# Reordering the pieces of pipelined local-attention layers, scores of one head unit beside values of another

## The reference

```python
def attn_layer(x, Wqkv, qs, ksc, Wo):
    q, k, v = jnp.split(x @ Wqkv, 3, -1)          # 16 heads of 64
    q = l2norm(q) * qs;  k = l2norm(k) * ksc
    q, k = rotary(q), rotary(k)
    sim = jnp.einsum('bhwie,bhwje->bhwij', q_windows, k_windows) * 8.0
    attn = jax.nn.softmax(where(mask, -max, sim), -1)      # 64 queries see 128 keys
    return merge_heads(attn @ v) @ Wo
def ffn_layer(x, g, bln, W1, b1, W2, b2):
    xn = layernorm(x) * g + bln
    a, gate = jnp.split(xn @ W1 + b1, 2, -1)      # 682 wide each
    return a * gelu(gate) @ W2 + b2
for i in range(6):
    x = attn_layer(shift_tokens(x), ...) + x
    x = ffn_layer(shift_tokens(x), ...) + x
```

## Time and profile before

| | |
|---|---|
| median of 3 runs | 3866.04 us (3858.51 to 3867.04) |
| profiled execution, span | 3864.4 us |
| PE, PEld busy in the span | 3676.7 us, 2617.3 us |
| DVE, ACT, POOL busy | 2739.6, 2354.5, 2226.1 us |
| local layers | from about 916 us to the end |

### The profile page before, as it was taken

The page is one execution under the profiler, slowest core; times in us unless marked ns, Lnnn a source line. Parts: engine busy times, 40 slices in busy tenths (PEclk is TensorE's granted clock), DMA queues, the critical chain, the costliest instruction groups (busy, mean ns, idle before and its releaser), DMA issues.

```text
span 3864.4 us, 79529 instructions
## 1 busy us (share of the span) xinstructions
PE 3676.7 (95%) x27354; PEld 2617.3 (68%) x27354; DVE 2739.6 (71%) x9052; ACT 2354.5 (61%) x6994; POOL 2226.1 (58%) x2087
## 2 busy tenths in 40 slices
PE   8899998867899999999999999999999999999998
PEld 6566666634567776777777777777777777777776
DVE  4688878744777777777777777777777777777763
ACT  3455555533566666666676666666666667666663
POOL 1677777763665655655556556565565555655640
PEclk9899999979999999999999999999999999999999
DMA  3777787780000001001000010000100001000000
GB/s 125 181 186 185 186 184 186 185 216 28 4 4 7 30 14 33 12 7 41 6 30 14 5 41 15 23 14 4 41 15 30 7 4 41 16 29 7 4 7 28
DMA packets 111071, 211.79 MB, mean 55 GB/s; under 512 B 22321, under 2 KB 72017, under 8 KB 109137
## 3 DMA queue, kind: packets, MB, share of 16 engines
q0 software_dynamic: 40960, 134.25, 14.7%
q1 hardware_dynamic: 69568, 72.33, 5.9%
q10 hardware_dynamic: 144, 0.13, 0.0%
HBM read 192.00 MB, written 2.10 MB: 50 GB/s over the span
## 4 chain that ended last, share of the span: by engine, by line
PE 70%; issue 2%; DVE 2%; POOL 1%; ACT 1%; DMA 0%; SPq 0%; DVEq 0%; POOLq 0%; ACTq 0%
PE pj L1818 24%; PE pj L1898 12%; PE y_ps L1881 8%; PE y_ps L1907 6%; PE sc L1846 5%; PE o_ps L1872 5%; PE tp L1857 5%; PE tp L1826 4%; PE tp L1796 1%; POOL l_qk_rot L1759 0%; DVE l_probs L2131 0%; DVE l_qk_cos L2092 0%; POOL l_r_q L1764 0%; DMA l_xf<-l_stream 0%; ACT l_probs L1977 0%
## 5 line engine op out<-in xcount | busy, mean ns | idle before, releaser
L1818 PE MATMUL pj<-w_qkv,l_xT 128*128 128x512 f32 x2304 | 1063.4, 598 | 7.3 <-ACT l_qk_sq L1964 5.8
L1759 POOL TENSOR_TENSOR l_qk_rot<-l_qk_cos,l_qk_sin 128x512 f32<-128x512 f32 x376 | 555.3, 1477 | 839.2 <-DVE l_qk_sin L2095 555.8
L1818 PEld LDWEIGHTS pj<-w_qkv,l_xT 128*128 128x128 f32 x2304 | 413.5, 191 | 387.1 <-issue 372.3
L511 POOL DMA_INDIRECT f_rows<-in_emb,f_expert x512 | 506.6, 989 | 224.9 <-issue 144.0
L1977 ACT ACTIVATE l_probs<-l_probs,l_low 128x128 f32<-128x128 f32 x1536 | 594.1, 391 | 2.2 <-DVE l_low L2131 0.4
L1898 PE MATMUL pj<-l_xnT,l_w 128*128 128x256 f32 x2112 | 511.4, 387 | 2.5 <-DVE l_hT L2162 1.2
L1942 ACT ACTIVATE l_qk_raw<-pj 128x512 f32<-128x512 f32 x384 | 227.1, 591 | 431.0 <-PE pj L1818 417.6
L2085 DVE TENSOR_REDUCE l_ss<-l_qk_sq 128x8 f32<-128x512 f32 x384 | 261.3, 680 | 312.7 <-ACT l_qk_sq L1964 167.9
L2131 DVE CUSTOM_DVE_ANT_0 l_probs<-sc,l_shut,l_r_q 128x128 f32<-128x128 f32 x1536 | 440.1, 343 | 52.7 <-PE tp L1857 45.8
L1898 PEld LDWEIGHTS pj<-l_xnT,l_w 128*128 128x128 f32 x2112 | 384.2, 191 | 65.5 <-issue 17.4
L1881 PE MATMUL y_ps<-w_o,l_oT 128*128 128x256 f32 x1536 | 339.6, 379 | 3.5 <-ACT l_oT L1942 3.5
...
## 6 DMA issues: line engine op xcount, KB each, us to landing
w_qkv<-in_L_ffn_Wqkv SPq DMA_DIRECT2D x12, 1024.0 KB, 7.1
...
f_rows<-in_emb,f_expert POOLq DMA_INDIRECT x512
w_o<-in_L_ffn_Wo SPq DMA_DIRECT2D x6, 1024.0 KB, 5.5
...
l_xf<-l_stream SPq DMA_DIRECT2D x48, 128.0 KB
...
```

The costliest lines, as they stand in the source:

```text
L511: pool.indirect_dma_start(rows[:, j % RH, k, :], None, dram["emb"], bass.IndirectOffsetOnAxis(ap=expert[:, n % 2, at:at + 1], axis=0)).the ...
L1759: pool.tensor_tensor(qk_rot[:, i % ROTS, :], qk_cos[:, b, :], qk_sin[:, b, :], ALU.add).then_inc(rotated if s == 0 else pool_front, 1)
L1818: last = pe.matmul(pj[b][:, :], xT[:, k, t * P:(t + 1) * P], w_qkv[:, k, s * INNER + c * 512:s * INNER + (c + 1) * 512], start=(k == 0), s ...
```

## The change

The four tables of the local layers are replaced by others. Nothing is computed otherwise, no instruction is added or removed, and no buffer or semaphore changes; `START` is empty in the changed kernel, so that step 0 uses the vector table too. The diff, cut to one line or two of each table (all line numbers behind the tables move up by 8):

```diff
     ORDER["tensor"] = [
-        ("project", 10, 0), ... ("scores", 0, 0), ("w1", 3, -3), ("w1", 4, -3), ("turn", (2, 1), -1), ("w1", 5, -3), ("turn", (2, 0), -1), ("values", 1, -1),
+        ("w1", 3, -3), ("w1", 4, -3), ("xs", 0, 1), ("w1", 5, -3), ("turn", (2, 1), -1), ("values", 1, -1), ("scores", 0, 0), ("turn", (2, 0), -1),
...
     ORDER["vector"] = [
-        ("rotate", 6, 0), ("rotate", 7, 0), ("turn", (1, 0), -1), ("top", (3, 0), -1), ("w1", 1, -3), ("res_a", 0, -2), ("qk_turn", 2, 0),
+        ("res_a", 0, -2), ("turn", (1, 0), -1), ("rotate", 6, 0), ("qk_turn", 2, 0), ("top", (3, 0), -1), ("w1", 1, -3), ("ln_stats", 0, -2),
...
-    START["vector"] = [
-        ("rotate", 3, 0), ("qk_turn", 0, 0), ("top", (2, 1), -1), ("rotate", 4, 0), ("turn", (0, 0), -1), ("rotate", 5, 0), ("norm", 1, -1),
```

More of the change, by code:

```diff
@@ L1411, in local_layers @@
     ORDER["tensor"] = [
[L1412 to L1415, removed]
@@ L1416, in local_layers @@
-        ("project", 0, 1), ("project", 1, 1), ("turn", (3, 1), -1), ("scores", 1, 0), ("turn", (3, 0), -1), ("project", 2, 1), ("values", 2, -1),
-        ("w2", 0, -3), ("qk_turn", 7, 0), ("w2", 1, -3), ("project", 3, 1), ("qk_turn", 6, 0), ("xn", 0, -2), ("values", 3, -1), ("turn", (0, 1), 0),
-        ("w1", 0, -2), ("scores", 2, 0), ("turn", (0, 0), 0), ("qk_turn", 0, 1),
+        ("turn", (0, 0), -1), ("project", 4, 0), ("qk_turn", 1, 0), ("project", 5, 0), ("project", 6, 0), ("wo", 0, -2), ("project", 8, 0),
@@ new lines, in local_layers @@
+        ("turn", (1, 0), -1), ("turn", (1, 1), -1), ("project", 7, 0), ("project", 9, 0), ("w1", 1, -3), ("qk_turn", 3, 0), ("qk_turn", 2, 0),
+        ("scores", 3, -1), ("values", 0, -1), ("w1", 2, -3), ("project", 10, 0), ("qk_turn", 4, 0), ("project", 11, 0), ("qk_turn", 5, 0),
+        ("w1", 3, -3), ("w1", 4, -3), ("xs", 0, 1), ("w1", 5, -3), ("turn", (2, 1), -1), ("values", 1, -1), ("scores", 0, 0), ("turn", (2, 0), -1),
+        ("project", 0, 1), ("turn", (3, 0), -1), ("turn", (3, 1), -1), ("project", 1, 1), ("values", 2, -1), ("scores", 1, 0), ("project", 2, 1),
@@ L1419, in local_layers @@
+        ("qk_turn", 6, 0), ("w2", 0, -3), ("qk_turn", 7, 0), ("project", 3, 1), ("xn", 0, -2), ("w2", 1, -3), ("turn", (0, 1), 0), ("qk_turn", 0, 1),
+        ("w1", 0, -2), ("values", 3, -1), ("scores", 2, 0),
     ]
     ORDER["scalar"] = [
-        ("o_copy", 3, -2), ("project", 4, 0), ("project", 5, 0), ("project", 6, 0), ("project", 8, 0), ("qk_turn", 1, 0), ("turn", (1, 1), -1),
-        ("project", 7, 0), ("project", 9, 0), ("exp", (2, 0), -1), ("w1", 1, -3), ("exp", (2, 1), -1), ("exp", (3, 0), -1), ("qk_turn", 3, 0),
@@ L1423, in local_layers @@
[L1423 to L1426, removed]
+        ("o_copy", 3, -2), ("qk_turn", 1, 0), ("exp", (1, 1), -1), ("project", 5, 0), ("project", 6, 0), ("project", 8, 0), ("exp", (2, 0), -1),
@@ new lines, in local_layers @@
+        ("project", 7, 0), ("turn", (1, 1), -1), ("project", 9, 0), ("w1", 1, -3), ("exp", (2, 1), -1), ("w1", 2, -3), ("qk_turn", 3, 0),
+        ("exp", (3, 0), -1), ("o_copy", 0, -1), ("project", 10, 0), ("project", 11, 0), ("w1", 3, -3), ("qk_turn", 5, 0), ("exp", (3, 1), -1),
+        ("w1", 4, -3), ("xs", 0, 1), ("w1", 5, -3), ("turn", (2, 1), -1), ("gelu", 0, -3), ("project", 0, 1), ("o_copy", 1, -1), ("project", 1, 1),
+        ("exp", (0, 0), 0), ("o_copy", 2, -1), ("turn", (3, 1), -1), ("exp", (0, 1), 0), ("project", 2, 1), ("qk_turn", 7, 0), ("xn", 0, -2),
@@ L1427, in local_layers @@
+        ("project", 3, 1), ("turn", (0, 1), 0), ("exp", (1, 0), 0), ("w1", 0, -2), ("project", 4, 1),
     ]
     ORDER["vector"] = [
-        ("rotate", 3, 0), ("qk_turn", 0, 0), ("top", (2, 1), -1), ("rotate", 4, 0), ("turn", (0, 0), -1), ("rotate", 5, 0), ("norm", 1, -1),
-        ("rotate", 6, 0), ("rotate", 7, 0), ("turn", (1, 0), -1), ("top", (3, 0), -1), ("w1", 1, -3), ("res_a", 0, -2), ("qk_turn", 2, 0),
-        ("top", (3, 1), -1), ("qk_turn", 4, 0), ("w1", 2, -3), ("norm", 2, -1), ("norm", 3, -1), ("w1", 3, -3), ("w1", 4, -3), ("ln_stats", 0, -2),
@@ L1432, in local_layers @@
-        ("w1", 5, -3), ("turn", (2, 0), -1), ("top", (0, 0), 0), ("ln_apply", 0, -2), ("top", (0, 1), 0), ("gates", 0, -3), ("rotate", 0, 1),
-        ("rotate", 1, 1), ("turn", (3, 0), -1), ("rotate", 2, 1), ("res_f", 0, -3), ("norm", 0, 0), ("qk_turn", 6, 0), ("top", (1, 0), 0),
-        ("top", (1, 1), 0), ("w1", 0, -2), ("top", (2, 0), 0), ("entry", 0, 2),
+        ("rotate", 3, 0), ("top", (2, 0), -1), ("turn", (0, 0), -1), ("rotate", 4, 0), ("norm", 1, -1), ("rotate", 5, 0), ("top", (2, 1), -1),
@@ new lines, in local_layers @@
+        ("res_a", 0, -2), ("turn", (1, 0), -1), ("rotate", 6, 0), ("qk_turn", 2, 0), ("top", (3, 0), -1), ("w1", 1, -3), ("ln_stats", 0, -2),
+        ("top", (3, 1), -1), ("w1", 2, -3), ("qk_turn", 4, 0), ("norm", 2, -1), ("rotate", 7, 0), ("w1", 3, -3), ("w1", 4, -3), ("entry", 0, 2),
+        ("w1", 5, -3), ("norm", 3, -1), ("top", (0, 0), 0), ("turn", (2, 0), -1), ("ln_apply", 0, -2), ("top", (0, 1), 0), ("rotate", 0, 1),
+        ("turn", (3, 0), -1), ("gates", 0, -3), ("rotate", 1, 1), ("top", (1, 0), 0), ("qk_turn", 6, 0), ("norm", 0, 0), ("top", (1, 1), 0),
@@ L1435, in local_layers @@
+        ("rotate", 2, 1), ("res_f", 0, -3), ("w1", 0, -2), ("qk_turn", 0, 1),
     ]
     ORDER["gpsimd"] = [
-        ("rotate", 3, 0), ("rotate", 4, 0), ("rotate", 5, 0), ("rotate", 6, 0), ("rotate", 7, 0), ("rope", 0, 1), ("ln_rstd", 0, -2),
-        ("rotate", 0, 1), ("rotate", 1, 1), ("rotate", 2, 1),
+        ("rotate", 6, 0), ("rotate", 7, 0), ("ln_rstd", 0, -2), ("rope", 0, 1), ("rotate", 0, 1), ("rotate", 1, 1), ("rotate", 2, 1),
+        ("rotate", 3, 1), ("rotate", 4, 1), ("rotate", 5, 1),
```

## The result

| | before | after |
|---|---|---|
| median of 4 runs each | 3862.93 us (3858.51 to 3867.04) | 3884.87 us (3881.26 to 3890.66) |
| ratio, 95% interval | | 1.0063 [1.0048, 1.0077] |
| span of the profiled execution | 3864.4 us | 3882.2 us |

The account below looks back on a forecast made before the run. TensorE, busy throughout the steady layers, was taken to bound the kernel. Span 3864.4 - 33 - 22 + 42 + 9 + 14 = 3874.4 us; with the median 1.6 above, 3876, stated as 3875, range 3836 to 3892.

Parts of the forecast that it names:

- Pairs: TensorE, steady steps: merging scores with values saves switches and restarts, 0.75 us a step, 33 us over 44 steps.
- Beginning and end: Fill, drain and last layer: TensorE waits less, as for scores behind top (1,1); 22 us off, bounds 0 and 35.
- Steady hand-offs: Ordinary steps: new order causes no waits between engines; 0 taken, bounds 0 and 0.4 us a step (0 to 18).
- hand-offs fail in each step: Rival, ordinary steps: hand-offs lose 0.2 to 0.4 us each step on top of the forecast; 3884 to 3893, chance 0.14.
- Late copy in a layer's last step: Five steps: staged copy queues behind next layer's loads, so project 11 is 8.5 us late, 42 us in all.
- lower bound: Layer's last step, if the copy overtakes the loads: project 11 late by only 4.0 us, 20 in all.
- Second step: Layer's second step, five times: copy stands behind Wo's 1 MB, late by 1.9 us, 9 us in all (bound 0).
- Clock: TensorE after the 8.5 us wait: lower granted clock costs 2.8 us, five times, 14 us (bounds 0 and 18).
- rival that nothing is late: Staged copy causes no lateness at all, so only the gains remain: 3866 - 55 = 3811 us; chance 0.07.

Follow-up runs that it names:

- e10: Kernel before with one pair merged: scores 1 moved behind turn (3,0) and project 2, to values 2; 3868.14 us (one run) against 3878.67, step 59.70 us.
- e4: e2 with two of the four merged pairs on TensorE pulled apart; 3951.35 us, 0.9958 of the kernel before.
- e7: e1 with both VectorE moves, those of e5 and e6; 3920.06 us, 0.9858 of the kernel before.
- e2: Changed kernel with the staged copy issued first in SP's step, ahead of both loads; 3932.68 us, 0.9910 of the kernel before.
- e1: Changed kernel with ln_stats back behind w1 4 on VectorE; 3928.14 us, 0.9887 of the kernel before.
- e5: e1 with VectorE's copy of turn (2,0) ahead of top (0,0); 3938.04 us (one run) against 3980.12 for the kernel before, step 59.47 us.
- e6: e1 with turn (3,0) and gates ahead of two rotate on VectorE; 3932.20 us (one run) against 3980.12 before, step 59.40 us.
- e3: Changed kernel with the staged copy issued after SP's wait for project 7 but ahead of the loads; 3958.03 us, 0.9983 of the kernel before.
- e8: Kernel before with values 3 moved behind turn (0,1) and w1 0, to scores 2; 4022.82 us (one run) against 3980.12, step 60.65 us.
- e9: Kernel before with scores 3 moved behind w1 1 and two transpose groups, to values 0; 3887.32 us (one run) against 3878.67, step 60.05 us.

## Why the prediction was right, and where its sizes were off

The forecast's mechanism is what happened, and the time fell into its range; the median is 10 us above the number. The forecast change was 9 us, the measured one 22 by the medians and 25.9 by the stack, since one step of the prediction failed. By its steps:

- **Pairs, 0.75 us a step: right.** e10 gives 0.15 for one pair that has transposes at its side, e4 0.37 for two, and e7, where only the hand-off ahead of qk_turn 3 is left (0.04), 59.85 - 59.15 + 0.04 = 0.74. 33 us.
- **Beginning and end, 22 us: right in sum.** From the first `xs` to the first wo it is 100.1 instead of 117.1 us, 17.0 less, though wo stands one project and four transposes later in the new order. The last two steps give 4.1 and the four steps of 60.4 that the kernel before has near its end 2.2; slower first steps and the end behind the last wo take 3.0 back: 20. The single cause named, scores waiting for `top` (1,1), is a small part: its wait fell from 5.1 us to 2.0. The clock, which this step did not name, is a larger one. The stretch from `xs` to wo, before and after (columns as above):

```profile
916.24:1033.33 117.09, 91.26 (x561) 50.34 (x561) 83.41 (x237) 60.69 (x177) 72.48 (x68) 0.89 0.07 23
...
908.09:1008.15 100.06, 85.73 (x568) 46.72 (x569) 85.94 (x233) 60.89 (x179) 73.73 (x69) 0.97 0.08 27
```

  TensorE's idle time fell by 11.5 us (25.8 to 14.3), and its busy time by 5.5 with more products to do, at a granted clock of 0.97 instead of 0.89. That the shorter waits brought the better clock is likely; no run takes the two apart. TensorE in the last steps after shows another late copy, in a step without loads, where few pieces are left to cover it:

```profile
3812.27 5.43 PE L1890 MATMUL pj<-l_xnT,l_w 128*128 128x256 f32 x12 [5.60 <-DVE l_hT L2154]
```

  e2, with the copy first in SP's step, waits there for 5.61 us too, so here it is the copy's own length that is not covered. e1 has no such wait, and its stack is 7.3 us shorter than e2's. That part was in no step of the prediction.
- **Steady hand-offs, 0: this step failed.** The wait it named as the closest, turn (3,1) behind the copy of turn (2,0), does not "hold by 0.2 to 0.3 us" but fails by 0.2. I let `top` (0,0) start in the moment in which TensorE had finished turn (2,0); it starts 0.46 us later. And I let TensorE start the moment the copy ends; it starts 0.14 later. The durations themselves were right. With `gates` (0.10 and 0.08) and qk_turn 3 (0.04) it makes 0.46 us a step, 20 us in all, just above the bound of 18. e5, e6 and e7 show it: with three of the four mended, a step is 59.15 us. This is the rival "hand-offs fail in each step", on top of the forecast, with a chance of 0.14, and the measured 3884.87 lies in its 3884 to 3893 as well as in the forecast's own range.
- **Late copy in a layer's last step, 8.5 us: measured 7.5 to 7.7** in the view of waits, 39 us in five steps by the starts, instead of 42. Loads were issued at 1800.98, 4.6 us after wo's end at 1796.41, as counted. `xf` came 19.65 after wo's end instead of 20.5. The lower bound, a copy that overtakes the loads, is ruled out by the DMA windows above and by e3: without loads ahead it came 15.01 us after wo's end (1907.26), 4.6 earlier. DMA: Bandwidth & Descriptors of the Trainium skill (Queues, rings and completion order) lets an engine take the descriptors of one ring in order. This case agrees: with the same tables TensorE waits 7.6 us when the copy stands behind 2 MB, 2.8 when it stands ahead of them, and never when it is the first of SP's step, and the windows show the weights pass before the copy.
- **Second step, 1.9 us: measured 0.8 to 1.1** of wait, 1.2 on average with what followed, 6 us instead of 9.
- **Clock, 2.8 us: measured 2.6**, 13 instead of 14.

The sum with the measured terms, 3864.4 - 33 - 20 + 20 + 39 + 6 + 13, is 3889.4; less the 8.1 us by which the unchanged first layers were quicker in this execution it is 3881.3, and the span was 3882.2. So the prediction was nearer than its steps: 20 us of hand-offs that it had left out, and 2 of the beginning and end, were met by 8 us of luck in code that the change does not touch, and by 7 us of late copies and clock counted too high.

The rival that nothing is late would have been faster by 55 us. e1 is that kernel, with hand-offs that still cost 20 us and 7 us gained in the last steps: its stack is 42 us shorter than that of before. e7, which mends most of the hand-offs too, has 65. What is settled is that the order on TensorE is worth its 33 us and that one place on VectorE costs 58 us, more than the 53 that pairs, beginning and end give: `ln_stats`, which can wait for a transfer, stands ahead of an instruction that gives a bank back to TensorE.

Not settled is why the first layers differ by 8 to 100 us between executions and chips; nothing of the change is in them. The one-run kernels (e5, e6, e8, e9, e10) rest on their step times, which repeat within 0.02 us in nearly all of some forty steps, and not on their totals.
